# Transposing a softmax's probabilities on VectorE in 32 by 32 blocks instead of on TensorE, and evicting the values' projections on ScalarE

## The reference

```
x = x + attn(layernorm(x));  x = x + ffn(layernorm(x))
attn: q, k, v = x @ Wq + bq, x @ Wk + bk, x @ Wv + bv       (8 heads of 128)
      scores = q k^T * 128**-0.5 within each block of 64 tokens
      out = softmax(scores) v;   return out @ Wo + bo
ffn:  h = relu(x @ Wfc^T)**2 (4096 wide);  y = h @ Wproj^T
      5 steps of mem = 0.9 mem + y - reset; return the share of steps that spiked
```

## Time and profile before

| | us |
|---|---|
| median of 3 runs | 709.12 (708.43 to 710.0) |
| the profiled execution's own time | 710.89 |
| its span on the slowest core (core 7) | 709.2 |
| spans of all cores | 705.4 to 709.2 |
| busy: TensorE, VectorE, ScalarE | 696.1, 384.1, 171.3 |
| block 0, block 1, block 2, block 3 start (scores) | 51.6, 124.7, 183.8, 243.0 |

### The profile page before, as it was taken

How to read it: one execution, slowest core, us unless ns; L and a number is a source line. 1 busy time by engine, 2 the same in 40 slices (tenths; PEclk the granted TensorE clock), 3 DMA queues, 4 the chain that set the end, 5 groups by cost and what they waited for, 6 DMA issues and landing times.

```text
span 709.2 us, 10652 instructions; the slowest of 8 cores (705.4 to 709.2 us)
## 1 busy us (share of the span) xinstructions
PE 696.1 (98%) x3804; PEld 325.6 (46%) x3804; DVE 384.1 (54%) x573; ACT 171.3 (24%) x314; POOL 49.4 (7%) x96
## 2 busy tenths in 40 slices
PE   8799999999999999999999999999999999999996
PEld 4444444444444444444444444444444444444444
DVE  5324866776587465337745226855225866221476
ACT  3454330451252036030003331002332001332000
POOL 2210210121005100000000000000000000000000
PEclk9999999999999999999999999999999999999999
DMA  8996976589559995496261002162002041100011
GB/s 181 213 154 137 156 152 196 123 199 220 147 173 187 235 240 93 127 185 189 87 210 59 1 1 60 58 198 85 16 1 61 34 144 74 45 1 1 30 44 45
DMA packets 31010, 80.92 MB, mean 114 GB/s; under 512 B 5616, under 2 KB 5872, under 8 KB 30192
## 3 DMA queue, kind: packets, MB, share of 16 engines
q0 software_dynamic: 12960, 31.46, 25.3%
q1 hardware_dynamic: 15552, 40.39, 19.2%
q10 hardware_dynamic: 2448, 8.40, 3.0%
HBM read 82.33 MB, written 16.78 MB: 140 GB/s over the span
## 4 chain that ended last, share of the span: by engine, by line
PE 94%; DMA 4%; DVE 1%; issue 1%; DVEq 0%; POOLq 0%
PE ps_m L416 31%; PE ps_y L488 30%; PE ps_m L363 14%; PE ps_m L389 8%; PE ps_m L403 8%; DMA wq_sb<-Wq 4%; DVE acc_sb L732 1%; PE ps_y L442 1%; PE ps_y L470 1%; PE ps_m L495 1%; PE ps_t L454 1%; DVE acc_sb L729 0%; PE ps_t L345 0%; DVE xr L737 0%; DVE attn_sb L747 0%
## 5 line engine op out<-in xcount | busy, mean ns | idle before, releaser
L416 PE MATMUL ps_m<-xn2t,w_sb 128*128 128x512 bf16 x1024 | 223.0, 379 | 0.1
L488 PE MATMUL ps_y<-w_sb,h_sb 128*128 128x512 bf16 (+1 forms) x1024 | 218.3, 376 | 0.0
L416 PEld LDWEIGHTS ps_m<-xn2t,w_sb 128*128 128x128 bf16 x1024 | 99.8, 98 | 119.3 <-issue 0.2
L488 PEld LDWEIGHTS ps_y<-w_sb,h_sb 128*128 128x128 bf16 x1024 | 100.2, 98 | 117.6
L574 ACT ACTIVATE h_sb<-ps_m 128x512 bf16<-128x512 f32 x128 | 76.4, 597 | 267.9 <-PE ps_m L416 267.9
L722 DVE TENSOR_TENSOR h_sb<-h_sb 128x512 bf16<-128x512 bf16 x128 | 53.1, 424 | 125.8 <-ACT h_sb L574 125.7
L732 DVE SCALAR_TENSOR_TENSOR acc_sb<-ps_y,acc_sb 128x1024 bf16<-128x1024 f32 (+2 forms) x72 | 78.6, 1092 | 7.9 <-DVE acc_sb L729 0.5
L363 PE MATMUL ps_m<-xnt,wq_sb 128*128 128x512 bf16 x240 | 58.4, 387 | 2.8 <-DMA wq_sb<-Wq 2.8
L363 PE MATMUL ps_m<-xnt,wk_sb 128*128 128x512 bf16 x248 | 58.6, 379 | 0.0
L389 PE MATMUL ps_m<-wv_sb,xnt 128*128 128x512 bf16 x256 | 56.9, 379 | 0.0
L403 PE MATMUL ps_m<-wo_sb,attn_sb 128*128 128x512 bf16 x256 | 55.9, 379 | 0.0
(11 more groups left out here) (63 smaller groups left out, 341.3 us busy)
## 6 DMA issues: line engine op xcount, KB each, us to landing
xr<-x SPq DMA_DIRECT2D x32, 512.0 KB, 6.4
xl<-x SPq DMA_DIRECT2D x96, 128.0 KB, 4.4
w_sb<-Wfc POOLq DMA_DIRECT2D x32, 256.0 KB, 8.4
x<-xr ACTq DMA_DIRECT2D x16, 512.0 KB, 4.1
out<-xr POOLq DMA_DIRECT2D x12, 512.0 KB, 2.9
w_sb<-Wpr POOLq DMA_DIRECT2D x16, 256.0 KB, 33.1
xn2t<-blk SPq DMA_DIRECT2D x64, 64.0 KB, 2.0
w_sb<-Wpr POOLq DMA_DIRECT2D x4, 1024.0 KB, 14.9
```

The lines of the kernel that those rows point to most:

```text
L416: m = E.matmul(bank(key)[:], w1_sb[fc // 4][:, k0:k0 + 128], tokens(xn2t, c, 0, 4), start=(c == 0), stop=(c == 7))
L488: return E.matmul(out, h_sb[fc][:, tt * 128:(tt + 1) * 128], w2_sb[fc // 4][:, k0:k0 + n], start=(fc == 0), stop=(fc == 31))
```

## The change

The probabilities of a pair are no longer transposed by TensorE. VectorE transposes them from `p_sb` to `pt_sb` with its block transpose: one instruction transposes each 32 by 32 block in its place on the partitions (this gives the diagonal blocks of each 64 by 64), and four more, one for each 32 partitions, write the off-diagonal blocks to the neighbouring 32 partitions, over what the first wrote there. The slots of this step are now 2, 6, 10 and 14 (13 in blocks 1 to 3), one after `softmax_scale`. `pt_sb` has four buffers, `p_sb` one. The first `values` of blocks 1 to 3 moves from slot 13 to slot 14, and `values` waits for `ve_pt` instead of the copies. The scores of the eight token blocks are put on other partitions (even ones on the lower 64, odd ones on the upper). ScalarE evicts v in `main`, and `v_copy` is gone from VectorE.

```diff
 def turn_p_pair(b, s):
-    slots = [9, 13, 17, 21] if b == 0 else [5, 9, 14, 17]
+    slots = [2, 6, 10, 14 if b == 0 else 13]
 def values_four(b, s):
-    slots = [16, 24] if b == 0 else [13, 18]
+    slots = [16, 24] if b == 0 else [14, 18]
...
-    p_sb = [at(f"p_sb_{i}", WORK + 57344 + 1024 * i, 512, BF16) for i in range(2)]
-    pt_sb = [at(f"pt_sb_{i}", WORK + 59392 + 1024 * i, 512, BF16) for i in range(2)]
+    p_sb = at("p_sb", WORK + 57344, 512, BF16)
+    pt_sb = [at(f"pt_sb_{i}", WORK + a, 512, BF16) for i, a in enumerate([58368, 59392, 60416, 96256])]
...
-                for bl in range(8):
-                    s0 = (h % 4) * 256 + (bl % 4) * 64
+                for bl in (0, 2, 4, 6, 1, 3, 5, 7):
+                    q0 = (bl % 2) * 64
+                    s0 = (h % 4) * 256 + (bl // 2) * 64
                     m = E.matmul(
-                        ps_s[(bl // 4) * 64:(bl // 4) * 64 + 64, s0:s0 + 64],
+                        ps_s[q0:q0 + 64, s0:s0 + 64],
...
-        def turn_p(p, j):
-            E.wait_ge(ve_p, 4 * p + j + 1)
-            turn_free(("pt", p, j))
-            for i in range(4):
-                m = E.transpose(ps_t[:, i * 128:(i + 1) * 128],
-                                p_sb[j % 2][:, i * 128:(i + 1) * 128], ident[:])
-            m.then_inc(full_t, 1)
-
         def values(p, f):
-            E.wait_ge(free_t, turn_no[("pt", p, 2 * f + 1)] + 1)
+            E.wait_ge(ve_pt, 4 * p + 2 * f + 2)
...
-                    p0 = (h % 2) * 256 + (bl % 4) // 2 * 128 + (bl // 4) * 64
+                    g = (h % 2) * 4 + bl // 2
+                    pt = pt_sb[h // 2][:].rearrange("p (b g t) -> p g b t", b=2, g=8)
...
-                                 pt_sb[h // 2 % 2][kb:kb + 64, p0:p0 + 64], start=True, stop=True)
+                                 pt[kb:kb + 64, g, :, :], start=True, stop=True)
...
+            elif key[0] == "v":
+                v0 = key[2] * 1024 + key[3] * 512
+                m = E.copy(v_sb[:, v0:v0 + 512], bank(key)[:])
...
-                if key[0] != "v":
-                    main(key)
+                main(key)
...
+            if p + j > 0:
+                E.wait_ge(ve_pt, 4 * p + j)
+            E.tensor_tensor(p_sb[:].rearrange("p (g k) -> p g k", g=8), e8,
...
-        def p_copy(p, j):
-            E.wait_ge(full_t, turn_no[("pt", p, j)] + 1)
-            E.tensor_copy(pt_sb[j % 2][:], ps_t[:, 0:512]).then_inc(free_t, 1)
-
-        def v_copy(key):
-            _, p, tt, half = key
-            E.wait_ge(*filled(key))
-            v0 = tt * 1024 + half * 512
-            E.tensor_copy(v_sb[:, v0:v0 + 512], bank(key)[:]).then_inc(emptied(key)[0], 1)
+        def p_turn(p, j):
+
+
+            blocks = p_sb[:].rearrange("p (g b t) -> p g b t", g=8, b=2)
+            turned = pt_sb[j][:].rearrange("p (b g t) -> p g b t", b=2, g=8)
+            if p > 0:
+                E.wait_ge(full_v, 4 * p - 2 + 2 * (j // 2))
+            E.wait_ge(ve_p, 4 * p + j + 1)
+            c = chained(E.transpose(turned, blocks))
+            E.wait_ge(ve_c, c)
+            for r in range(4):
+                half, to = r % 2, r // 2 * 2 + 1 - r % 2
+                m = E.transpose(turned[32 * to:32 * to + 32, :, half, :],
+                                blocks[32 * r:32 * r + 32, :, 1 - half, :])
+            m.then_inc(ve_pt, 1)
```

More of the change, by code:

```diff
@@ L156, in turn_order @@
                 keys.append(("x", i))
-            if (j := turn_p_pair(b, s)) is not None:
-                keys.append(("pt", b, j))
     return {k: n for n, k in enumerate(keys)}
@@ L270, in build_nc @@
     ve_var, ve_xn, ve_p, ve_sq = sem("ve_var"), sem("ve_xn"), sem("ve_p"), sem("ve_sq")
+    ve_pt = sem("ve_pt")
     ve_bqs, ve_eps, ve_out = sem("ve_bqs"), sem("ve_eps"), sem("ve_out")
@@ L509, in tensor_program @@
                     turn_x(i)
-                if (j := turn_p_pair(b, s)) is not None:
-                    turn_p(b, j)
                 if (f := scores_four(b, s)) is not None:
@@ L690, in softmax_scale @@
             E.wait_ge(ve_c, c)
-            E.tensor_tensor(p_sb[j % 2][:].rearrange("p (g k) -> p g k", g=8), e8,
+            if p + j > 0:
+                E.wait_ge(ve_pt, 4 * p + j)
+            E.tensor_tensor(p_sb[:].rearrange("p (g k) -> p g k", g=8), e8,
                             rsum[:].unsqueeze(2).broadcast_to([128, 8, 64]),
                             ALU.mult).then_inc(ve_p, 1)
-        def p_copy(p, j):
-            E.wait_ge(full_t, turn_no[("pt", p, j)] + 1)
-            E.tensor_copy(pt_sb[j % 2][:], ps_t[:, 0:512]).then_inc(free_t, 1)
-        def v_copy(key):
-            _, p, tt, half = key
-            E.wait_ge(*filled(key))
-            v0 = tt * 1024 + half * 512
-            E.tensor_copy(v_sb[:, v0:v0 + 512], bank(key)[:]).then_inc(emptied(key)[0], 1)
+        def p_turn(p, j):
[11 more added lines that the diff above has]
+            m.then_inc(ve_pt, 1)
         def add_bo(p, tt):
@@ L764, in vector_program @@
                 if (j := turn_p_pair(b, s)) is not None:
-                    p_copy(b, j)
+                    p_turn(b, j)
                 if (i := ln_unit(b, s, LN_SCALE)) is not None:
@@ L773, in vector_program @@
                     softmax_scale(b, j)
-                if key[0] == "v":
-                    v_copy(key)
                 if b == 3 and s > 0:
```

## The result

The changed kernel takes 722.75 us (median of 4 runs, 721.05 to 724.39) against 709.39 us for the kernel before on the same chip: a ratio of 1.019, 95% interval 1.0174 to 1.0207. That is 13.4 us slower. I forecast slower, but by 3.4 us, and the time lies 7 us above the top of my range.

The account below looks back on a forecast made before the run. TensorE, busy 98% of the span, was taken as the bound. Its saving of 3.5 us against waits of 3.4 us in each of blocks 1 and 2 gave +3.4 us: 709.1 to 712.5 us, range 705.6 to 715.8.

Parts of the forecast that it names:

- TensorE's saving: TensorE's stream loses 16 groups of transposes at 0.22 us each, 3.5 us in all, with nothing taking their place.
- The wait for shift 3: Blocks 1 and 2: first values wait for VectorE's subtraction into e_sb, behind three turns, 2.7 us (1.6 to 3.9); chance 0.55.
- X: VectorE's time to turn one pair's probabilities, one large and four small block transposes: 2.67 us, from 2.29 to 3.05.
- 20.54 + 3X: Blocks 1 and 2: when shift 3 ends, counted from the start of the scores; 28.55 us with X at 2.67.
- 3X - 5.29: Blocks 1 and 2: TensorE's wait ahead of the first values, as a formula; 2.7 us at X of 2.67.
- The two small waits: Blocks 1 and 2: TensorE waits for ScalarE evictions queued behind VectorE, at slots 12 and 16: 0.46 and 0.25 us.
- S: Waits per block in blocks 1 and 2, 2.72 + 0.46 + 0.25 = 3.4 us; from 2.0 to 5.0.
- Blocks 0 and 3: nothing: The turns fit in VectorE's idle time in blocks 0 and 3, no wait; at the high X perhaps 0.3 us in block 3.
- Hidden after all: Rival: the turns fit in VectorE's idle time, only the 3.5 us saving stays, 705.6 us; chance 0.15.
- Break-even: Rival: small transposes overlap fully, blocks 1 and 2 lose about what TensorE saved, 708 to 710.5 us; chance 0.2.
- Slow reads of the new layout: Rival: values' matmuls read two short runs slowly, up to twice 0.58 us a set, +8.0 us, 717.1; chance 0.07.
- ScalarE in block 0: Rival: ScalarE bounds block 0, where values' projections stand behind exponentials, adding about 1 us; chance 0.03.

Follow-up runs that it names:

- the last three runs: e10, e8 and e9, measured on one chip, where the kernel before took 709.08 us.
- e9: Changed kernel with 13 added matmuls ahead of the first values of blocks 1 and 2, and all early Wproj loads held back until block 3's tile landed: 714.73 us.
- e8: Changed kernel with all early Wproj loads (tiles 0 to 3) held back until the transposed tile for block 3 has landed: 717.81 us, ratio 1.0123.
- e10: The changed kernel as it is, measured again on the chip of e8 and e9: 720.63 us, ratio 1.0165.
- e3: Changed kernel with 13 added matmuls, results overwritten, filling TensorE's wait ahead of the first values of blocks 1 and 2: 717.9 us, ratio 1.0125.
- e2: Changed kernel without the four small VectorE transposes between neighbouring partitions (output wrong): 706.68 us, ratio 0.9968.
- e1: Kernel before with only the values' projections' evictions moved to ScalarE: 709.23 us, ratio 0.9994.
- e5: Changed kernel with the four small transposes in two groups, each within one set of 32 partitions (output wrong): 721.1 us, ratio 1.0154.
- e6: Changed kernel with only the second half of the early Wproj loads (tiles 2 and 3) held back until block 3's tile landed: 722.72 us, ratio 1.0174.
- e4: Changed kernel with blocks 1 and 2 given back TensorE's transposes and old order; VectorE turns only in blocks 0 and 3: 707.5 us, ratio 0.9969.
- e7: Changed kernel with the turn of pair 2 moved behind shift 3 in blocks 1 to 3 (slot 12 instead of 10): 721.95 us, ratio 1.015.

## Why the prediction was right in direction and too small

On the chip of the last three runs the loss of 11.55 us divides by these medians, whose runs spread by 0.8 to 2.1 us, into

- **5.65 us (e9 against before)**: TensorE's waits for VectorE and ScalarE, less its saving;
- **3.1 us (e8 less e9)**: the lower clock after the wait;
- **2.8 us (e10 less e8)**: the late tile of block 3, with the clock fall behind it.

The order does not matter much: by their ratios, the added matmuls alone (e3 against e10) give 2.8 us. Without clock and tile the change would have taken 714.7 us (e9), inside my range.

**TensorE's saving: right.** 0.89 us a block where nothing waits (e2), 3.6 in all; I had 3.5. The new layout costs nothing (e2). The evictions cost nothing (e1).

**The wait for shift 3: right in place and form, X a little too small.** The sum of the first turn is 130.09 - 126.66 - 0.61 = 2.82 us, and the product into the single `p_sb` starts 0.17 after the reciprocal instead of 0.11, which makes 2.88 against my 2.67. The Trainium skill's rule on the start of an instruction in another partition group ("VectorE: DVE Perf Modes", "Two Vector instructions with no wait between them") holds here: starts 0.45 apart at 0.44 each where the group changes, 0.37 apart where it stays (e5). The 2.61 that I had put beside it left out the 0.08 us by which the product no longer overlaps what follows, 0.02 us more for each small transpose, and the wait for `p_sb`. My formula 20.54 + 3X gives 29.2 with the measured X, and shift 3 ended at 150.65 - 121.46 = 29.2 (VectorE's timeline below). With it 3X - 5.29 is 3.35. The values started at 150.80, 29.34 from the scores and 3.5 later than the 25.83 of my sum; the other 0.15 lies between the end of the shift and the first values' matmul, a step that I had put at nothing. The idle times in brackets add up to less, 0.46 + 2.83 = 3.3: they count from the end of the last matmul, while groups that do not wait overlap (1.89 us long, 1.73 apart). The first 0.46, for the bank of slot 8, only used up slack.

```profile
149.96 0.69 DVE L673 TENSOR_TENSOR e_sb<-ps_y,nmax 128x512 f32<-128x512 f32 x1
150.57 0.68 DVE L644 BATCH_NORM_STATS2 stat<-xl 128x6 f32<-128x512 f32 x1
```

**The two small waits: right in the main.** In block 2 TensorE waits for shift 3, then for the bank of slot 12, then for that of slot 16:

```profile
214.35 0.64 PE L463 MATMUL ps_y<-pt_sb,v_sb 64*128 64x64 bf16 x32 [2.82 <-DVE e_sb L673]
...
217.48 1.89 PE L362 MATMUL ps_m<-xnt,wk_sb 128*128 128x512 bf16 x8 [0.65 <-ACT q_sb L558]
...
225.51 8.79 PE L388 MATMUL ps_m<-wv_sb,xnt 128*128 128x512 bf16 x40 [0.29 <-ACT v_sb L566]
```

I had 0.46 and 0.25, counted from start to start; so counted, with the lost overlap of 0.16, they are 0.81 and 0.45 here. Per block S is 62.67 - 59.16 + 0.89 = 4.4 us in block 1 and 4.8 in block 2, where I had 3.4; with the measured X my own sum gives 3.35 + 0.46 + 0.46 = 4.3, and with the 0.15 4.4. This term, mis-sized mainly through X, is 2.3 us of what I missed (5.65 against 3.4). The 0.4 us by which block 2 is longer than block 1 is the wait for the bank of slot 12: at full clock it is 0.29 us in block 1 and 0.65 in block 2 (e3 and e9, every core). Why it differs I did not follow.

**"Blocks 0 and 3: nothing": wrong for block 3, and this is one step that failed.** Two things were missed. Small: on most cores a third wait for shift 3, 0.3 to 0.4 us (block 3 gains 0.5, not 0.9). Large: the tile. I checked the tile that block 2 needs, found 12 us to spare, and let it stand for both. SyncE's queue for block 3's tile in the kernel before was (first row; block 3 starts at 243.0), and in the changed one (second fence):

```profile
220.80 11.38 SPq L938 DMA_DIRECT2D xn2t<-blk  x16
```

```profile
229.85 11.04 SPq L937 DMA_DIRECT2D xn2t<-blk  x16
```

The times from issue to landing of these 16 transfers, before (core 7), changed (core 6) and in e8 (core 0):

```profile
DMA to landing us min/median/max: 6.1/6.3/7.8
...
DMA to landing us min/median/max: 6.9/7.6/12.7
...
DMA to landing us min/median/max: 2.6/5.9/8.2
```

Before, the last of the 16 transfers was issued by 232.2, 10.8 us ahead of block 3, and landed at 238.5; TensorE first used the tile at 243.85, so there were 5.3 us to spare. On the other cores it was 2.6 to 6.3 us, and on core 0, with the least, the last transfer took 10.7 us. In the changed kernel (core 6) the last is issued by 240.9, 7.2 us ahead of the scores at 248.05, and takes 12.7 us, where that of core 7 before took 6.9. So the issue has come 3.6 us closer and the landing takes 5.8 us longer, together more than the 5.3: the tile lands 4.1 us too late. e8 shows the second half of the cause: with 4 MB of Wproj loads out of the way the same late issues land in time; with only the later half of them out of the way (e6) they do not. Which of the first eight loads it is that delays them, and why some cores are hit and others are not, stays open; it was not tried. Nor is the longer landing all due to VectorE: in e2, where no turn is late, the last transfer already takes 9.5 to 13.3 us, against 6.7 to 10.7 before. On core 6, the slowest, block 3 is 5.2 us longer than before, of 14 in all; by the medians of the slowest core it is 2.8 (e10 less e8), so a step that touches few cores still shows in a metric of the slowest.

**The clock: a step that was not in the working at all.** I priced a wait at its length. e3 shows that it is not: at full clock block 1 is 62.67 us; as it ran, it took 63.1 to 64.3, and some cores show a weaker, later fall too: on cores 0 to 3 of the profiled execution, and on none of cores 4 to 7, the granted clock is at 0.81 for some 5 us, from 14 to 20 us after a wait on. I had read the clock of the earlier trace rows as 1.00 and not asked what a pause would do to it.

**The rivals.** Hidden after all: out, since every core waits; the busy sum over the stretch (26.4 us of work for 25.8) had spoken against it rightly. Break-even: out, since the small transposes do not overlap in the changed kernel, and the first turn took 2.8 us and not 2.29. Slow reads of the new layout: out by e2. ScalarE in block 0: out, block 0 gained 0.9 everywhere. None of my rivals contained the tile or the clock, and so the range ended at 715.8. Of the signs that I named, TensorE's busy time fell by 1.7 us and not by 3.5, partly because a group of matmuls at the lower clock lasts longer (3.36 us instead of 1.90).

## What to carry to other kernels

Take work off the bound engine only in the stretches where the other engine is idle: the same turns are worth 0.9 us a block where VectorE has time and cost 3.5 us or more a block where it has not (e4 against the changed kernel). When an in-order engine gets late, follow everything that it releases to its next deadline, in each stage by itself, DMAs and queues included; moving one item in its queue only moves the wait (e7). And price a new pause of TensorE above its length, as its clock may fall behind it (after 12 of 16 waits of 2.8 us here).

## What the hardware showed that I had not expected

- Four transposes of 32x256 that each start on other partitions are 0.45 us apart at 436 ns each; on the same partitions the second starts 0.37 after the first (e5).
- After 2.8 us without a matmul the granted clock is sometimes, not always, at 0.5 of full speed for 3.4 us (on core 6 after the pause in block 1, and not after the equal one in block 2). In e7, where the longest pause of blocks 1 and 2 is 2.04 us, it still fell after 5 of 16 such pauses. 13 filler matmuls prevented it on all cores and gave back 3.1 us by medians (e8 less e9).
- The last 64 KB transfer of the tile took 6.7 to 10.7 us to land in the kernel before, 8.7 to 12.7 in the changed one, beside 4 MB of weight loads, and 3.2 to 5.7 with these loads held back (e8).
- ScalarE's copy of a values' projection takes 589 ns where VectorE took 685 for it:

```profile
L566 ACT CAST v_sb<-ps_m 128x512 bf16<-128x512 f32 x32 | 18.7, 589 | 22.4 <-PE ps_m L388 22.3
```
